# Attention over 13 key tiles: rounds of two tiles, with PSUM banks from a table over seven

## The reference

```
x = x + cross_attention(layernorm(x), ctx, ctx)   # 16 heads of 16; ctx has 1601 rows per sequence
x = x + causal_self_attention(layernorm(x))       # 16 heads of 16, within the 64 tokens
x = x + moe(layernorm(x))                         # 8 experts 256 -> 1024 -> 256, gelu, top 2 of 8
# cross attention, per batch and head:
scores = (q @ k.T) / sqrt(16);  out = softmax(scores) @ v;  out @ Wo.T + bo
```

## Time and profile before

| | us |
|---|---|
| three runs, median (lowest to highest) | 671.48 (670.67 to 673.57) |
| the profiled execution | 674.92 |
| its span (first to last instruction) | 673.1 |
| PE busy in it | 647.2 (96%) |
| DVE, ACT, POOL busy | 473.2 (70%), 326.8 (49%), 298.4 (44%) |
| chain that ended last | PE 79%, DVE 10%, issue 5%, POOL 3%, ACT 2% |
| mean granted TensorE clock | 0.989 of full speed |

### The profile page before, as it was taken

One profiled execution on the slowest core, in us unless ns is written; L12 is line 12 of the kernel. 1 busy time (PEld: TensorE's weight loads), 2 busy tenths in 40 slices (PEclk: granted clock), 3 DMA queues, 4 the chain that ended last, 5 costly groups with the idle time before them and its releaser, 6 DMA issues.

```text
span 673.1 us, 15769 instructions
## 1 busy us (share of the span) xinstructions
PE 647.2 (96%) x6408; PEld 533.3 (79%) x6408; DVE 473.2 (70%) x871; ACT 326.8 (49%) x533; POOL 298.4 (44%) x386
## 2 busy tenths in 40 slices
PE   7989999999999999999999999888999999999997
PEld 4778878778778868877886876657789999999997
DVE  4887767676759778476877864768778677667753
ACT  4355655654554554554455544345554444444431
POOL 2147787997766788596668757100000000000000
PEclk9999999999999999999999999878999999999999
DMA  5311110100110010110001000153003303320001
GB/s 177 135 50 50 39 39 26 51 26 25 27 50 2 26 52 25 26 51 25 27 25 26 1 2 1 33 220 127 1 1 126 115 12 125 125 98 26 0 0 33
DMA packets 13285, 34.12 MB, mean 51 GB/s; under 512 B 1563, under 2 KB 10532, under 8 KB 11044
## 3 DMA queue, kind: packets, MB, share of 16 engines
q1 hardware_dynamic: 13188, 33.19, 14.8%
q0 software_dynamic: 32, 0.01, 0.0%
HBM read 32.67 MB, written 0.52 MB: 49 GB/s over the span
## 4 chain that ended last, share of the span: by engine, by line
PE 79%; DVE 10%; issue 5%; POOL 3%; ACT 2%; DMA 0%; POOLq 0%; DVEq 0%; ACTq 0%
PE bank L1169 45%; PE bank L1363 9%; PE bank L1178 9%; PE bank L1349 4%; PE bank L1239 3%; POOL prob_sum L482 3%; PE bank L1282 2%; PE bank L1291 2%; DVE maxes L883 2%; DVE prob_sum L482 2%; DVE ctx_lo L466 1%; DVE shift L825 1%; ACT k_hi L618 1%; PE bank L1266 1%; DVE k_lo L864 1%
## 5 line engine op out<-in xcount | busy, mean ns | idle before, releaser
L482 POOL TENSOR_TENSOR prob_sum<-probs,prob_sum 128x256 f32<-128x256 f32 x336 | 268.5, 831 | 72.1 <-ACT probs L722 66.7
L722 ACT ACTIVATE probs<-bank 128x1024 f32<-128x1024 f32 (+1 forms) x104 | 106.7, 1026 | 115.3 <-PE bank L1363 103.2
L883 DVE TENSOR_REDUCE maxes<-bank 128x1 f32<-128x400 f32 (+1 forms) x256 | 129.5, 565 | 21.7 <-PE bank L1239 21.3
L704 ACT ACTIVATE h_raw<-bank,b_sb 128x512 f32<-128x512 f32 (+2 forms) x72 | 46.2, 642 | 107.0 <-PE bank L1169 106.9
L1169 PE MATMUL bank<-w_hi,h_hi 128*128 128x256 f32 x256 | 72.6, 284 | 0.0
L1169 PE MATMUL bank<-w_hi,h_lo 128*128 128x256 f32 x256 | 72.1, 282 | 0.0
L1169 PE MATMUL bank<-w_lo,h_hi 128*128 128x256 f32 x256 | 72.0, 281 | 0.0
L1178 PE MATMUL bank<-probs,v_sb 128*32 128x128 f32 (+1 forms) x1664 | 68.3, 283 | 2.5 <-DVE masked L815 2.0
L864 DVE SCALAR_TENSOR_TENSOR k_lo<-bank,bias_sb,k_hi 128x400 fp32r<-128x400 f32 (+2 forms) x64 | 40.4, 631 | 43.0 <-ACT k_hi L618 42.8
L1169 PE MATMUL bank<-wv_hi,ctx_hi 128*128 128x256 f32 (+1 forms) x208 | 65.4, 314 | 2.7 <-DVE maxes L883 2.4
L1363 PE MATMUL bank<-qbd_hi,k_hi 64*128 64x256 f32 (+1 forms) x416 | 67.9, 322 | 0.0
(11 more groups left out here) (158 smaller groups left out, 1422.0 us busy)
## 6 DMA issues: line engine op xcount, KB each, us to landing
raw<-in_w SPq DMA_DIRECT2D x16, 1024.0 KB, 6.8
ctx_raw<-in_ctx_t SPq DMA_DIRECT2D x16, 400.0 KB, 3.6
ctx_raw<-in_ctx_t SPq DMA_DIRECT2D x8, 402.0 KB, 3.6
ctx_raw<-in_ctx_t SPq DMA_DIRECT2D x8, 399.0 KB, 3.6
w_sb<-in_w_t SPq DMA_DIRECT2D x1, 1280.0 KB
w_raw<-in_w_t SPq DMA_DIRECT2D x2, 256.0 KB, 4.7
result<-x_all SPq DMA_DIRECT2D x4, 128.0 KB, 2.0
x_all<-in_x SPq DMA_DIRECT2D x1, 384.0 KB, 4.2
```

The costliest lines, as they stand in the source:

```text
L482: ins = engine.tensor_tensor(prob_sum[0:ROWS[k], cols], probs[0:ROWS[k], s % 2, cols], acc[0:ROWS[k]], ALU.add)
L704: nc.scalar.activation(h_raw[:, c % 2, 0:width], bank[:, at, 0:width], ACT.Gelu, bias=b1_sb[:, bass.ds(e, 1), c:c + 1].rearrange("p a b -> ...
L722: nc.scalar.activation(probs[0:ROWS[k], s % 2, :].rearrange("p (g n) -> p g n", g=G), bank[0:ROWS[k], score_bank(b, k):score_bank(b, k) + ...
L883: nc.vector.tensor_reduce(maxes[:, g * PAIRS + j, c:c + 1], src[:, 0:width], AX.X, ALU.max).then_inc(read_dve, 1)
```

## The change

The steps of a batch are taken in rounds: (0, 1), (2, 3), ... (10, 11) and 12 alone. Only the last batch stays at one step a round. In a round PE makes: the first pair of M, the scores of the first tile, its other M pair, the scores of the second tile, its M pairs, then all other units of both steps, then `weigh` of both steps (before: of the step before). Scores of even k lie in banks 0 and 1, of odd k in 2 and 3, in all batches. The first M pair of a round goes into banks 2 and 3, so ahead of the second tile's scores; later pairs into (4, 5), (6, 4), (5, 0). The units behind the scores go through a table by the number of M pairs, which takes in the score banks that the exponentials have read. `wait_banks` waits for whatever used a bank last, units or exponentials.

DVE takes, per round: `chain_between` for what the round before left, the spreading of the next queries, the M reductions of both steps, `find_shift` (now in the round of k = 11), `split_lo`, then the other units step by step. ACT takes both exponentials, then the units. POOL waits for `inverse_root`'s input ahead of the sum of the round's second step. `probs` has three buffers instead of two, `prob_sum` two instead of one (so the first sum of a batch no longer waits for the denominators of the batch before). `M_AT` moves later (steps 2 to 11 instead of 1 to 9), V 0 comes at step 2, X behind the scores of step 12. In the last tile's table most chain units come one step later.

```diff
-RING_BANKS = range(2, 7)
-LATE_BANKS = range(4, 7)
+MAXIMA_BANKS = [(2, 3), (4, 5), (6, 4), (5, 0)]
+BANKS_BEHIND = {0: [4, 5, 6, 0, 1, 2, 3], 3: [0, 1, 5, 2, 3, 6, 4], 4: [1, 2, 3, 6, 4, 5, 0]}
+BANKS_SINGLE = [2, 3, 5, 6, 4]
+BANKS_LAST = [4, 5, 6]
+PROB_BUFFERS = 3
-V_AT = {3: [0, 1]} | {k: [k - 2] for k in range(4, KT)}
+V_AT = {k: [k - 2] for k in range(2, KT)}
-M_AT = in_order({1: 2, 2: 2, 3: 2, 4: 1, 5: 2, 6: 2, 7: 1, 8: 2, 9: 2})
+M_AT = in_order({2: 2, 3: 1, 4: 2, 5: 1, 6: 2, 7: 1, 8: 2, 9: 2, 10: 2, 11: 1})
+SPLIT_LO_AT = {4: 2, 8: 6, 10: 8, 12: 11}
-REST_CHAIN = {3: ["p1"], 5: ["r1"], 6: ["p2"], 8: ["r2"], 9: ["p3"], 11: ["r3"], 13: ["bias"]}
+REST_CHAIN = {4: ["p1"], 5: ["r1"], 6: ["p2"], 7: ["r2"], 8: ["p3"], 9: ["r3"], 13: ["bias"]}
-FIND_SHIFT_AT = KT - 3
+FIND_SHIFT_AT = KT - 2
...
+def score_banks(k):
+
+    return range(ROW_TILES * (k % 2), ROW_TILES * (k % 2) + ROW_TILES)
...
+            for s, (m, _) in zip(steps, rows):
+                self.front[s] = []
+                ahead = ROW_TILES if s == steps[0] else 0
+                for kind, u in m[:ahead]:
+                    self.front[s].append(take(kind, u, next(maxima)))
+                if own:
+                    self.users.append((tuple(score_banks(s % KT)), "scores", s))
+                for kind, u in m[ahead:]:
+                    self.front[s].append(take(kind, u, next(maxima)))
```

On POOL:

```diff
+            def tile(t, units, more):
+                for steps in units.rounds:
+                    for s in steps:
+                        bi, k = divmod(s, KT)
+                        if s == steps[-1]:
...
+                            if "y1" in kinds:
+                                inverse_root(2 * t + 1)
+                            if "y2" in kinds:
+                                inverse_root(2 * t + 2)
+                        if not more == bi == 1:
+                            sum_probabilities(nc.gpsimd, pool, 2 * t + bi, k, SUM_PIECES)
```

On DVE:

```diff
             def tile(t, units, more, chain):
+                for steps in units.rounds:
+                    first_bi, first_k = divmod(steps[0], KT)
+                    paired = len(steps) > 1
+                    if chain and paired:
+                        chain_between(units, steps[0], t - 1)
+                    if first_k == 0 and more > first_bi:
+                        next_batch_queries(2 * t + first_bi, first_bi)
+                    for s in steps:
+                        for m, kind, u in units.front[s]:
+                            unit(units, m, kind, u, t - 1, 2 * t + first_bi + 1, (first_bi + 1) % 2)
...
+                    for s in steps:
...
+                        if k == 1 and not is_first(b):
+                            dve.wait_ge(denom_done, b)
+                            at = (bi + 1) % 2 * Q
+                            own_heads(bank[:, O, :], o_read, b)
+                        if more == bi == 1:
+                            sum_probabilities(nc.vector, dve, b, k, 1)
+                        for m, kind, u in units.at[s]:
+                            unit(units, m, kind, u, t - 1, b + 1, (bi + 1) % 2)
+                        if k == 1 and not is_first(b):
+                            divide_heads(o_t[:, :, at:at + Q], o_ready)
+                        after_units(units, s)
+                        if chain and not (paired and s == steps[0]):
+                            chain_between(units, s, t - 1)
```

On PE:

```diff
             def tile(t, units):
+                for steps in units.rounds:
...
+                    for s in steps:
+                        k = s % KT
+                        ahead = ROW_TILES if s == steps[0] else 0
+                        for n, kind, u in units.front[s][:ahead]:
+                            unit(units, n, kind, u, t - 1, b + 1, (bi + 1) % 2)
                         shift_scores(units, b, bi, k)
+                        scores(b, bi, k)
+                        for n, kind, u in units.front[s][ahead:]:
+                            unit(units, n, kind, u, t - 1, b + 1, (bi + 1) % 2)
+                    for s in steps:
+                        if s % KT == 1 and not is_first(b):
+                            denominators(b - 1)
+                        for n, kind, u in units.at[s]:
+                            unit(units, n, kind, u, t - 1, b + 1, (bi + 1) % 2)
+                    for s in steps:
+                        k = s % KT
+                        if not last_batch:
+                            weigh(b, k)
+                        elif k >= 2:
+                            weigh(b, k - 1)
```

More of the change, by code:

```diff
@@ new lines, in wait_banks, with wait_free @@
+    def wait_banks(self, eng, sems, banks, user):
+        for sem, count in zip(sems, map(max, zip(*[self.read_before(bank, user) for bank in banks]))):
+            if count > 0:
+                eng.wait_ge(sem, count)
+    def wait_free(self, eng, sems, n):
+        if n == 0 and self.previous is None and self.before[1]:
+            eng.wait_ge(sems[1], self.before[1])
+            eng.wait_ge(sems[2], self.before[2])
+        user = next(i for i, (_, what, m) in enumerate(self.users) if what == "unit" and m == n)
+        self.wait_banks(eng, sems, [self.bank[n]], user)
@@ L155, in counts, with wait_scores @@
+    def wait_scores(self, eng, sems, s):
+        user = next(i for i, (_, what, m) in enumerate(self.users) if what == "scores" and m == s)
+        self.wait_banks(eng, sems, self.users[user][0], user)
     def counts(self, n):
@@ L658, in step @@
                 for n, kind, u in units.at[s]:
-                    if not (kind == "X" and units is not PROLOGUE):
-                        unit(units, n, kind, u, t, b, parity)
+                    unit(units, n, kind, u, t, b, parity)
             def prepare(k):
@@ L736, in _ @@
+            for t in range(TT - 1):
+                tile(t, TILES[t], 2)
             tile(TT - 1, LAST, 1)
@@ L1052, in tile @@
                         dve.wait_ge(read_dve, units.before[2] + units.counts(n + 1)[2])
                         find_shift()
-                    for m, kind, u in units.at[s]:
-                        unit(units, m, kind, u, t - 1, b + 1, (bi + 1) % 2)
-                    if k == 1 and not is_first(b):
-                        divide_heads(o_t[:, :, at:at + Q], o_ready)
-                    after_units(units, s)
-                    if chain:
-                        chain_between(units, s, t - 1)
@@ L1443, in _ @@
+            for t in range(TT - 1):
+                tile(t, TILES[t])
             tile(TT - 1, LAST)
-            weigh(B - 1, 1, KT - 1)
+            weigh(B - 1, KT - 1)
             denominators(B - 1)
```

329 lines of the change are left out of this document (144 added, 185 removed).

## The result

The changed kernel takes **682.05 us** (median of 4 runs, 679.93 to 684.82), the kernel before on the same chip 672.53 (4 runs, 670.67 to 674.72): ratio 1.0143, 95% interval [1.0111, 1.0175], 9.5 us slower. The forecast was 684.6.

What follows compares the result with a forecast made beforehand. PE's stream was taken to bound batches 0 to 6; -17.6 for merges plus 7.7, 13.3, 5.4, 3.4 and 0.9 for waits, clock and POOL gave +13.1 us on 671.5: 684.6 us, 8-in-10 range 667 to 693.

Steps and rivals of the forecast that it cites:

- 42 merges: Six merged steps in each of 7 batches save PE's tile-shape switches, 0.42 us each: -17.6 us.
- wait of every head: PE waits for DVE to reduce the M pair in banks 2 and 3, 0.22 us in 35 rounds: +7.7 us.
- divide_heads: Left from round (0, 1), it makes DVE 0.50 us late at round (2, 3), batches 1 to 6: +3.0 us.
- y1, y2: Steps 3 and 18: `normalize` ahead of the M reductions makes DVE late by 1.26 us, batches 2 to 5: +5.0 us.
- s0: Round (8, 9): DVE late by 1.4 us in batches 2 and 4, some 0.6 in batch 6: +3.4 us.
- route: Routing is DVE's last work in round (8, 9); PE waits 5.0 us in batches 3 and 5, less old waits: +5.4 us.
- batch's end (POOL): Batches 0 and 1: `denominators` waits for POOL's last sum; two merges' worth taken back, +0.9 us.
- clock: The `route` waits bring PE's clock down, some 3.4 us at half speed, twice: +3.4 us.
- lateness terms: DVE late at round heads through work left from the round before, terms from `divide_heads` to s0: 13.3 us in all.
- Rival 3: POOL sets each batch's end, all five last sums taking the slow form: 15 us more, 700 us; chance 0.05.
- the second: Rival: half of the lateness, route and clock terms is hidden, 673.6 us, no change that can be told; chance 0.20.
- rival 1: DVE is in time at round heads, only 0.22 us a round left and old waits gone: 658 us; chance 0.14.

Runs made afterwards that it cites:

- e1: The changed kernel with no M pair ahead of the first tile's scores and none in banks 2 and 3: 671.9 us, ratio 0.9981.
- e2: The changed kernel with DVE's `chain_between` of a round's first step behind the M reductions instead of ahead: 676.98 us, ratio 1.007.
- e3: e1 with each step's weigh behind its own units, so two single weighs a round: 680.83 us, ratio 1.0135.
- e7: e6 with the last tile's exponentials of batches 0 and 1 taken into the denominators by PE: 668.85 us, ratio 0.9954.
- e6: e5 with the first M pair put between the second tile's shift rows and scores: 672.27 us, ratio 1.0007.
- e8: e5 with PE taking POOL's last sum in batches 0 and 1, two M pairs in round (8, 9), four in (4, 5), (6, 7): 668.45 us.
- e10: e8 with the gates' transpose and the b2 term two key tiles later in the last batch: 665.13 us, ratio 0.9877.
- e9: Changed kernel with PE taking POOL's last sum in batches 0 and 1, two M pairs in round (8, 9), four in (4, 5), (6, 7): 677.25 us.
- experiment 2: Three kernels built on e1 to find its missing gain: e5 669.42 us, e6 672.27 us, e7 668.85 us.
- e5: e1 with other bank tables only, second M pair in banks (6, 4), third in (0, 1): 669.42 us, ratio 0.9954.

## Why the prediction was right, and what was mis-sized

The direction came out for the stated reason: the new waits cost more than the merges save, and e1, e2 and e3 show both sides. That the sum came within 2.6 us of the measured time is in part luck: single terms were off by up to 4.4 us, in both directions, and cancelled. Term by term, measured in the profiled execution after, whose mean clock is that of the profiled one before (0.990 and 0.989):

| term | forecast | measured |
|---|---|---|
| 42 merges | -17.6 | 0.34 each (e3; round 7.75 to 7.62 with 0.21 of wait in it): -14.3 |
| wait of every head | +7.7 | 0.21 to 0.22 each: +7.7 |
| `divide_heads` | +3.0 | +2.5; batch 0 has +1.7 besides, where DVE takes layer-norm statistics and two `ctx_lo` ahead of the reductions |
| y1, y2 | +5.0 | 0.89 to 0.90 each: +3.6 |
| o0, o1 | +0.8 | +0.4 |
| `qbd` | +1.1 | +0.4 |
| s0 | +3.4 | 1.03, 1.05 and 0.43: +2.5 |
| `route` | +5.4 | head 1.62 and front 0.99, twice, less 4.2: +1.0 |
| batch's end (POOL) | +0.9 | waits of 0.78 and 2.37: +3.1 |
| clock | +3.4 | +4.2, by the runs at their own clocks |

The measured terms without the clock add up to +8.6, and at equal clock the kernel is 5.3 slower. By batch: batches 0 to 6 are 4.6 us longer in the profiled executions. The terms would give 8.6, less 2.2 for two waits of the kernel before that went as well and that I had not counted (1.43 at 47.5 us, 0.74 at 141.1), plus some 3 for the two stretches at half clock (batch 5 has one and is 1.5 longer than batch 3): 9.4. Most of the difference lies in batch 6: it is 4.0 us shorter (62.13 to 58.11) although its merges give 2.0 and its heads take 1.9 back. Of these 4.0, 2.2 are work that moved: o0 and o1 take PE from 420.63 to 422.87 before, and stand one step later after, in the last batch; another 0.8 are waits around s1 and st10 that got shorter. The last batch and the experts take the same time in both, 248.7 and 249.0, but after has 6.8 us less at half clock there, worth up to 3.4 (an estimate: half of it). So the moved work was probably paid there and hidden by the clock; no run tests it by itself. I had counted the last batch at nothing and not looked for work that goes there.

- **The base wait came out**, 0.21 to 0.22 where I had 0.22. Both sides of the difference were 0.08 to 0.09 short: DVE's is 1.59 (107.83 to 109.42) where I had 1.51, PE's own 1.38 where I had 1.29.
- **The lateness terms were right in place and a third too long.** They stood where forecast, round by round; PE's round is 0.08 longer for each merge than I had it, which takes that much off each term. The rest of the difference I have not taken apart.
- **`route` was the mis-sized term.** I took from the earlier trace rows that the routing ends 11.2 after its step's head. After, DVE goes from the reciprocal at 243.38 to the copy at 246.72 in 3.34 us, where it was 4.39; and PE doesn't arrive 5 us early, since the M pairs ahead of that head stop first: their banks are read by ACT, which stands behind the router's row maximum on DVE. A wait that an earlier wait of the same engine takes up is not paid twice; only the sum counts, 1.84 + 0.40 + 0.59.
- **POOL** was placed right (batches 0 and 1) and taken too small: I let it cost two merges' worth and missed that PE's whole round gets shorter, so that 2.37 stand at 144 us with a half clock behind them. Removing it gave 3.4 us in the medians (e7 against e6). Rival 3 in its strong form (every batch) didn't come; PE waits for POOL in two places only.
- **The clock.** The forecast had it behind `route`; of two such stretches in batches 0 to 6 one came there (362 us), the other began inside POOL's wait. What is shown: runs of one kernel at a lower mean clock are slower, by 0.4 to 0.6 us for each 0.001 in most kernels (e1 and e7 show 0.3, and e1 has spans of 668.1 and 671.2 at the same 0.986); in batches 0 to 6 of the profiled executions every low stretch begins inside a PE wait of 1.3 to 2.4 us or within 1.9 us behind its end; with such waits taken out of batches 0 to 6 (e8, e10: none above 0.71) no low stretch is left there. What stays open is what decides whether one comes. It is not the size of the wait: e9 waits 2.32 and 2.29 us in its routing rounds and has no low stretch in batches 0 to 6. In e7 the same wait of 1.57 stands in both routing batches, and only the second is followed by half clock:

```profile
237.00:241.00 4.00, 2.79 (x36) 2.38 (x40) 3.90 (x9) 1.46 (x5) 3.86 (x6) 1.00 0.02 4
350.00:354.00 4.00, 4.00 (x51) 3.11 (x51) 3.93 (x6) 1.66 (x4) 3.14 (x4) 0.57 0.00 0
```

Of the rivals, the first and the second needed DVE to hide half or more of the lateness; of the 13.3 us only 4 did not come. e1 reached rival 1's condition at the heads by other means and took 671.9, not 658: a bank held, waits for `maxes` elsewhere (experiment 2), 3.3 less from the merges, and clocks of 0.983 to 0.989 where the kernel before has mostly 0.995.

The Trainium skill's page "GPSIMD Engine Reference" (its table of the engine: GpSimd contends with VectorE instructions of two SBUF inputs) was cited in the forecast for a rival. The trace of the kernel before agrees, and more sharply than the forecast read it. Of the six pieces from 293.17 on, the first three stand beside DVE's reductions and take 0.72 each, the other three stand beside `ctx_lo`, `shift` and `qbd`, which have two SBUF inputs, and take 1.61 each:

```profile
293.17 2.15 POOL L482 TENSOR_TENSOR prob_sum<-probs,prob_sum 128x256 f32<-128x256 f32 x3 [0.90 <-ACT probs L722]
```

```profile
295.27 4.84 POOL L482 TENSOR_TENSOR prob_sum<-probs,prob_sum 128x256 f32<-128x256 f32 x3
```

Of all 364 pieces of that trace, 261 have no such instruction beside them and take 0.72 on average; 29 have one beside nine tenths or more of their time and take 1.25. (What ran beside what is read off the times; no run changes it alone.) What the rival made of it did not come: the mean over all pieces is 0.81 before and 0.82 after.

## What to carry to other kernels

Merging steps saves the switches of TensorE's tile shape, 0.34 us each here, but a bank that is filled, read by another engine and filled again within the merged round costs more than that; put the reused bank last in the round, and no pair where its reader hasn't ended. Such a wait needn't show as idle time: compare the distance between starts in a cluster with that of the same instructions elsewhere. When the stream gets denser, look at what each run's clock does before believing a small gain or loss: e5 had the shorter stream and gave a part of it back. And when a step is moved, look at the batch that it moves into.

## What the runs showed of the hardware

- A short wait of TensorE can cost more than itself: half clock for 3.4 us came with waits of 1.34 (e5) and 2.37 us (after), for 10.2 us with one of 3.46 (e8). It does not come each time: e9's waits of 2.32 and 2.29 us had none. Within one kernel, e5, spans lie from 662.4 us at a mean clock of 0.991 to 671.1 at 0.976.
- The second of two matmuls that run side by side in the array's halves can be held by its bank while the first goes on: starts at 107.482, 107.636, 107.662 and 107.923 in e1, where e5 has two pairs 0.18 apart. The profile shows PE as busy all the time.
- A group of 16 weigh products takes 0.46 us when its kind follows and 0.58 when another shape does, before and in e3; in e3 the K pass behind it takes 0.28 where its followers take 0.18.
- GpSimd's sum of 128x256 takes 0.72 us on average with no two-input SBUF instruction of VectorE beside it, 1.25 with one beside nearly all of it (kernel before).
